# First stage of a four-stage decoder block kernel: a new order of a batch, and six of sixteen odd states summed by accumulating DMAs

## The reference, cut to what matters

```python
x = einsum('bld,ed->bel', hidden_states, in_proj_w)      # 512 channels
x = silu(causal_conv4(x) + conv_b)                       # u
dt_low, Bm, Cm = split(einsum('bdl,ed->bel', x, x_proj_w), [16, 32], axis=1)
dt = softplus(einsum('brl,dr->bdl', dt_low, dt_proj_w) + dt_proj_b)   # delta
def step(state, inp):                                    # 16 states a channel
    d, b, c, u = inp
    state = state * exp(d[..., None] * A) + (d * u)[..., None] * b[:, None, :]
    return state, einsum('bdn,bn->bd', state, c)
y = scan(step) + D[None, :, None] * x
y = y * silu(z)                                          # z is the layer-normalized input
```

## Time and profile before

| | |
|---|---|
| median of 3 runs | 3984.52 us (3982.64 to 3984.68) |
| the profiled execution's own time | 3983.86 us |
| its span | 3982.3 us |
| PE busy | 3702.0 us (93%) |
| DVE busy | 2985.4 us (75%) |
| ACT busy | 1753.5 us (44%) |
| POOL busy | 643.9 us (16%) |
| first scan of the first stage | starts at 62.8 us |
| DVE multiply L1763 that closes a batch | 256.95, ..., 646.40 and 804.93 us |

### The profile page before, as it was taken

How to read it: one execution, slowest core, us unless ns; L and a number is a source line. 1 busy time by engine, 2 the same in 40 slices (tenths; PEclk the granted TensorE clock), 3 DMA queues, 4 the chain that set the end, 5 groups by cost and what they waited for, 6 DMA issues and landing times.

```text
span 3982.3 us, 40913 instructions
## 1 busy us (share of the span) xinstructions
PE 3702.0 (93%) x12733; PEld 1922.2 (48%) x12786; DVE 2985.4 (75%) x4787; ACT 1753.5 (44%) x2732; POOL 643.9 (16%) x595
## 2 busy tenths in 40 slices
PE   7898898899999998899999999999999999999787
PEld 4555555544444444444446444455454455454343
DVE  5788888888979787888988655577377277377397
ACT  5767676742323323344342111155255255254276
POOL 2233232233434110244421000000000000000000
PEclk9999998999999999999999999999999999999898
DMA  4232222333242322434335000211011021021000
GB/s 139 76 108 78 102 96 82 139 139 137 82 160 100 119 79 91 162 143 161 126 109 227 22 22 21 88 65 66 29 65 57 29 74 52 32 71 70 0 11 32
DMA packets 91724, 344.89 MB, mean 87 GB/s; under 512 B 11776, under 2 KB 20096, under 8 KB 78112
## 3 DMA queue, kind: packets, MB, share of 16 engines
q1 hardware_dynamic: 63040, 230.05, 16.2%
q0 software_dynamic: 28512, 112.74, 8.4%
HBM read 280.36 MB, written 62.39 MB: 86 GB/s over the span
## 4 chain that ended last, share of the span: by engine, by line
PE 58%; DVE 22%; issue 11%; ACT 6%; DMA 2%; DVEq 0%; ACTq 0%; POOL 0%; SPq 0%; POOLq 0%
PE ps L1121 39%; PE ps L1499 5%; PE ps L1199 3%; PE ps L1330 3%; PE ps L1489 3%; PE ps L1382 3%; DVE room L1662 2%; DVE room L1666 2%; DVE room L1670 1%; ACT room L806 1%; DMA room<-bc_scratch 1%; PE ps L1189 1%; DVE stat L1626 1%; DVE room L1688 1%; DVE room L1675 1%
## 5 line engine op out<-in xcount | busy, mean ns | idle before, releaser
L1121 PE MATMUL ps<-room 128*128 128x512 bf16 (+2 forms) x3001 | 964.7, 478 | 54.7 <-DVE xres L2155 17.9
L1121 PE MATMUL ps<-lnT,room 128*128 128x512 f32 x2240 | 985.5, 595 | 23.5 <-DVE room L1871 15.1
L1121 PEld LDWEIGHTS ps<-lnT,room 128*128 128x128 f32 x2240 | 425.4, 191 | 567.7 <-issue 528.3
L1121 PEld LDWEIGHTS ps<-room 128*128 128x128 bf16 (+1 forms) x3040 | 422.1, 142 | 573.0 <-issue 318.5
L636 POOL TENSOR_TENSOR idle<-idle 128x1 f32<-128x1 f32 x268 | 468.2, 1747 | 1326.2 <-ACT room L816 508.6
L1330 PE MATMUL ps<-room 128*128 128x512 f32 x864 | 377.9, 595 | 7.3 <-DVE room L1822 7.3
L743 ACT ACTIVATE room<-room,small 128x511 f32<-128x511 f32 x256 | 163.6, 710 | 367.1 <-DVE room L1666 367.0
L1719 DVE TENSOR_TENSOR_SCAN room<-room 128x2048 f32<-128x2048 f32 x64 | 283.2, 4425 | 10.8 <-ACT room L806 4.7
L1666 DVE TENSOR_TENSOR_SCAN room<-room 128x2048 f32<-128x2048 f32 x64 | 283.4, 4428 | 5.4
L2115 DVE TENSOR_REDUCE stat<-ps 128x1 f32<-128x512 f32 x256 | 177.1, 692 | 132.1 <-PE ps L1121 132.1
L1330 PEld LDWEIGHTS ps<-room 128*128 128x128 f32 x864 | 164.2, 191 | 213.1 <-issue 207.3
(11 more groups left out here) (226 smaller groups left out, 4889.0 us busy)
## 6 DMA issues: line engine op xcount, KB each, us to landing
room<-in_ffn SPq DMA_DIRECT2D x16, 2048.0 KB, 10.6
room<-bc_scratch POOLq DMA_DIRECT2D x128, 256.0 KB, 3.6
room<-kv_stash SPq DMA_DIRECT2D x64, 512.0 KB, 3.4
kv_stash<-room POOLq DMA_DIRECT2D x96, 256.0 KB, 2.3
room<-stash POOLq DMA_DIRECT2D x24, 1024.0 KB, 5.6
room<-in_ffn SPq DMA_DIRECT2D x20, 1024.0 KB, 5.8
room<-in_ffn SPq DMA_DIRECT2D x12, 1536.0 KB, 7.5
room<-in_head SPq DMA_DIRECT2D x68, 256.0 KB, 3.7
```

What stands on the lines that cost most here:

```text
L1121: last = nc.tensor.matmul(out, lhsT, rhs, start=(i == 0), stop=(i == len(parts) - 1))
```

## The change

- **Order ahead of the loop.** SP loads the context and the first weight block before the small constants. Set 1's weights come after the key weights, and the delta weights have a semaphore of their own. x of the last batch is loaded only when the last batch begins. Columns of C are turned after delta is made. Only four units of keys and values are made ahead, one of them (2) before the first decay. Two one-column activations of Exp (`load_exp`) stand where the next real Exp is some work away.
- **Convolutions in pairs.** Two channel blocks go through all four taps, then the other two. `conv_done` and `u_ready` count to two each, silu and the 48-row projection follow by pairs.
- **Order in a batch.** On ACT the copies of state n come ahead of most side work of that n. Silu of set 1 and `take_xd` move to n = 2, the delta pieces and the Exp of set 1 one place earlier, silu of set 0 from n = 8 to 6, its Exp from 11 to 9, its Ln from 13 to 10, silu of z from 15 to 10. On DVE softplus of set 1 moves from 7 to 6, the convolution of set 0 from 5 to 6, the layer norm from 9 to 8, the delta*u pair from 10 to 9, softplus of set 0 from 12 to 10.
- **Keys and values.** Units sit at the states of `KV_ORDER`; two states (6 and 8) have two. Eight units use this batch's context from the loaded copy, four use the block loaded for the input projection. The last batch has eight units.
- **Single stores.** D*u is stored at n = 8, delta*u at 11, delta at 13, with a semaphore of its own for the first.
- **Accumulating DMAs.** States 1, 3, 5, 7, 9 and 11 are not summed on PE. Their turned copies go to one 1 MB buffer (`m_acc`: x's place for the last batch, or `m_nd` in the last batch), and POOL sends it to a DRAM tensor, the first as a plain store and the others with an addition. After state 12 POOL loads the sum back, and PE adds it with four matmuls at n = 14.

```diff
-KV_HEADS, KV_LEAD = 12, 6
+KV_HEADS, KV_LEAD = 12, 4
+ACC = (1, 3, 5, 7, 9, 11)
+ACC_LOAD, ACC_AT = 12, 14
+ACC_SUMMED = sum(n not in ACC for n in range(ACC_AT)) + 1
+SUMS = DS - len(ACC) + 1
+KV_OWN = KV_HEADS - KV_LEAD
+KV_ORDER = (4, 5, 6, 6, 7, 8, 8, 9, 10, 11, 12, 13)
...
+            sp.dma_start(ctx[:, :], ctx_d[0:P, :]).then_inc(ctx_loaded, 16)
+            sp.dma_start(mws[0][:, 0:MW], min_d[0:P, :]).then_inc(mw_loaded[0], 16)
             sp.dma_start(small[:, :], small_d).then_inc(small_loaded, 16)
...
+                    if last:
+                        sp.wait_ge(nsum_done, (B - 2) * SUMS + ACC_SUMMED)
+                        load_x(B - 1)
...
-                            sp.wait_ge(tile_filled, tile("kv", KV_HEADS - KV_LEAD - 1, 1)[0] + 1)
+                            sp.wait_ge(tile_filled, tile("kv", KV_OWN - 1, 1)[0] + 1)
                             sp.dma_start(m_kctx, ctx_d[bass.ds(b * P + P, P), :]).then_inc(kctx_loaded, 16)
...
+                        if n == 8:
+                            place = stashed(2, b)
+                            sp.wait_ge(Du_ready, b + 1)
+                            sp.dma_start(place, m_zT).then_inc(Du_stored, 16)
+                        if n in (11, 13):
+                            place = stashed((n == 11) * 1, b)
                             sp.wait_ge(stash_ready, b + 1)
+                            sp.dma_start(place, m_u2 if n == 11 else m_nd2).then_inc(stash_stored, 16)
...
-                sp.wait_ge(stash_stored, B * 48)
+                sp.wait_ge(stash_stored, B * 32)
+                sp.wait_ge(nsum_done, (B - 1) * SUMS + ACC_SUMMED)
+                sp.wait_ge(Du_stored, B * 16)
...
+                for n in range(DS):
+                    if n in ACC:
+                        if n > ACC[0]:
+                            pool.wait_ge(acc_added, b * (len(ACC) * 16) + ACC.index(n) * 16)
+                        wait(tile_taken, tile("h", n, NT - 1)[0] + 1, count)
+                        count += 1
+                        pool.dma_start(acc_stash, m_acc[last] if n % 2 else m_hT,
+                                       accum_op=ALU.add if n > ACC[0] else ALU.bypass).then_inc(acc_added, 16)
+                    for i in kv_slots(n, last):
+                        if i is not None:
+                            h = (KV_LEAD + i) % KV_HEADS
+                            place = kv_stashed(b + (1 if i >= KV_OWN else 0), h)
+                            store_unit(place, [tile("kv", i, half)[0] for half in range(2)], count,
+                                       None if last and i + 2 >= slots else (h + 2) % KV_HEADS, i)
+                            count += 2
+                    if n == ACC_LOAD:
+                        wait(acc_added, b * (len(ACC) * 16) + len(ACC) * 16, count)
+                        count += 1
+                        pool.dma_start(m_acc[last], acc_stash).then_inc(acc_loaded, 16)
...
+                    for pair in range(2):
+                        act.wait_ge(conv_done, 2 * f + (pair + 1))
+                        for e in (2 * pair, 2 * pair + 1):
+                            last_u = nc.scalar.activation(u3[:, e, :], u3[:, e, :], ACT.Silu, bias=cb[:, e:e + 1])
+                        last_u.then_inc(u_ready, 1)
...
+                        if n in (4, 5):
+                            take_dt(1, n - 4, tile)
+                        if n == 8 and not last:
+                            act.wait_ge(sp_corrected, front_b + 1)
+                        if n in (8, 9) and not last:
+                            take_dt(0, n - 8, tile)
+                        turned = t3(m_acc[last] if n in ACC and n % 2 else m_hT, NT)
+                        sent = sum(m in ACC for m in range(n - 1))
+                        if n - 2 in ACC and (n in ACC or n % 2 == 0):
+                            act.wait_ge(acc_added, b * (len(ACC) * 16) + sent * 16)
+                        for t in range(NT):
+                            i, bank = tile("h", n, t)
+                            act.wait_ge(tile_filled, i + 1)
+                            nc.scalar.activation(turned[:, t, :], ps[:, bank, :], ACT.Copy,
+                                                 scale=cT3[:, t, DR + DS + n:DR + DS + n + 1]).then_inc(tile_taken, 1)
+                        early, late = kv_slots(n, last)
+                        if early is not None:
+                            take_kv(early, b * (KV_HEADS * 16) + (KV_LEAD + early) * 16, tile)
+                        if n == 2:
                             silu_u(front_b, 1)
                             if not last:
                                 take_inproj(0, front_a, tile)
+                            take_xd(front_b, 1, b, tile)
                         if n == 5:
+                            exp_abs(1, tile)
+                        if n == 6 and not last:
+                            silu_u(front_a, 0)
+                        if late is not None:
+                            take_kv(late, b * (KV_HEADS * 16) + (KV_LEAD + late) * 16, tile)
                         if n == 6:
+                            ln_w(front_b)
+                            if not last:
+                                take_xd(front_a, 0, b + 1, tile)
...
+                        if n == 9 and not last:
+                            exp_abs(0, tile)
+                        if n == 10:
                             if not last:
+                                ln_w(front_a)
+                            act.wait_ge(Du_stored, b * 16 + 16)
                             for t in range(NT):
...
+                        if n == ACC_AT:
+                            pe.wait_ge(acc_loaded, b * 16 + 16)
+                            for t in range(NT):
+                                mm = nc.tensor.matmul(ps[:, t, :], ident[:, :], t3(m_acc[last], NT)[:, t, :], start=False, stop=False)
+                            mm.then_inc(nsum_done, 1)
+                        if n not in ACC:
+                            for t in range(NT):
+                                pe.wait_ge(tile_taken, tile("h", n, t)[0] + 1)
+                                mm = nc.tensor.matmul(ps[:, t, :], ident[:, :], hT3[:, t, :], start=(n == 0), stop=(n == DS - 1))
+                            mm.then_inc(nsum_done, 1)
...
-                    for j in range(DC - 1, -1, -1):
-                        for e in range(NE):
+                    for pair in range(2):
+                        for j in range(DC - 1, -1, -1):
+                            for e in (2 * pair, 2 * pair + 1):
...
                         if n == 2:
-                            dve.wait_ge(stash_stored, b * 48)
+                            dve.wait_ge(stash_stored, b * 32)
                             convolve(front_b, 1, tile)
-                        if n == 5 and not last:
-                            dve.wait_ge(Du_summed, b + 1)
-                            convolve(front_a, 0, tile)
-                        if n == 7:
+                        if n == 6:
                             softplus(front_b, 1)
+                            if not last:
+                                dve.wait_ge(Du_summed, b + 1)
+                                convolve(front_a, 0, tile)
```

More of the change, by code:

```diff
@@ L34, with kv_slots @@
 NBC = 2
[L37 to L44 removed]
+KV_HEADS, KV_LEAD = 12, 4
[5 more added lines that the diff above has]
+KV_ORDER = (4, 5, 6, 6, 7, 8, 8, 9, 10, 11, 12, 13)
+def kv_slots(n, last):
+    slots = [i for i, at in enumerate(KV_ORDER) if at == n and not (last and i >= KV_OWN)]
+    return (slots + [None, None])[:2]
 def mamba_tiles(last):
@@ L51, in mamba_tiles @@
     for n in range(DS):
+        early, late = kv_slots(n, last)
         names += [("h", n, t) for t in range(4)]
-        if kv_slot(n, last) is not None:
-            names += [("kv", kv_slot(n, last), half) for half in range(2)]
+        if early is not None:
+            names += [("kv", early, half) for half in range(2)]
         if n == 0:
@@ L652, in store_kv @@
                 tile = batch_tiles(b, last)
[L653 to L659 removed]
+                slots = KV_OWN if last else KV_HEADS
+                count = b * KV_WAITS + KV_FIRST
+                for n in range(DS):
[17 more added lines that the diff above has]
+                        pool.dma_start(m_acc[last], acc_stash).then_inc(acc_loaded, 16)
             def store_late(k):
@@ L1745, in body @@
                             v.tensor_tensor(m_u2, m_nd2, m_u2, ALU.mult).then_inc(stash_ready, 1)
-                        if n == 12 and not last:
+                        if n == 10 and not last:
                             softplus(front_a, 0)
```

192 lines of the change are left out of this document (83 added, 109 removed).

## The result

The changed kernel took **4008.56 us** (median of 4 runs, 4006.19 to 4014.7), the kernel before 3983.58 beside it: ratio **1.0068**, interval [1.0055, 1.008]. It is slower by 0.7% where 1.5% less was forecast; 4008.56 lies outside the range. The profiled execution took 4014.7 us, 0.15% above the median.

What follows compares the result with a forecast made beforehand. PE was taken as nearest to a bound, its lateness showing in DVE's waits. Gains of 14.7 ahead of the loop, 38.7 in three batches and 7 in the last sum to 60.4, giving 3923 us, range 3884 to 3974.

Steps and rivals of the forecast that it cites:

- The waits named above go: Loop batch: with sums taken off PE, four DVE waits totalling 25.4 us vanish, leaving 169.3 of 194.7 us at best.
- the closing 9.5: DVE's 9.5 us wait at L1763, closing a batch, for PE's last sums; claimed to go.
- the 4.8 for ACT's Ln of set 1: DVE's 4.8 us wait at L1743; claimed to go because that Ln moves three states ahead of its user.
- the 7.3 for row 11: DVE's 7.3 us wait for a row of B, read as PE's lateness through the context load; claimed to go.
- 181.8 - 6: Loop batch: forecast of 181.8 us, less the 6 us charged for the additions.
- +6.5, ACT late at the softplus of set 0: States 6 to 9: DVE waits 9.3 us for ACT's Exp, some 3 replacing an old wait, so 6.5 us a batch more.
- the new order does not do what it says: Rival, in the loop: batches stay near 194 us, only the stretch ahead and part of the last gained; 3964 us, chance 0.05.
- The additions, 9 us landing and 6 us a batch: POOL's queue: additions land in 9 us, key stores behind them delay ACT, costing 6 us a batch.
- The last batch, -7: Last batch: PE 11 us less, no ACT wait, 3 charged for the next stage's late weights; net gain 7 us.
- Ahead of the loop, 14.7 (9 to 18): Before the first scan: earlier weights, pairs, turned C after delta, Exp table and later keys together gain 14.7 us.
- the signs: Trace marks foretold: first scan at 48 us, L1763 some 182 apart, PE near 154, 88 sum records, row 11 unwaited.
- PE at its slower clock again the last releaser at L1763: Refuting sign at the batch's closing multiply; the others were additions beyond 14 us and ACT's copies waiting for acc_stash.

Runs made afterwards that it cites:

- e7: Changed kernel with the six odd states summed nowhere (missing from y) and no DMA for them; 3981.1 us, ratio 0.9989.
- e16: e9 with the sums of states 1, 3, 5, 7, 9 and 11 made nowhere, no DMA added; 3968.6 us, ratio 0.9962.
- e9: e3 with four leading units, late units reading the projection's context block, and the key context load at n = 14 instead of 10; 3960.8 us, ratio 0.9942.
- e1: Changed kernel with all sixteen states summed on PE and no accumulating DMAs; 3981.8 us, ratio 0.9998.
- e3: Kernel before with only the new stretch ahead of the loop and the pairs; old batch order, six leading units, no additions; 3964.5 us, ratio 0.9959.
- e5: Changed kernel with its additions turned into plain stores of the same size, so part of y is left out; 3992.9 us, ratio 1.0017.
- e8: Changed kernel with accumulating DMAs in the first three batches only, the last batch summing all states on PE; 3992.3 us, ratio 1.0016.
- e4: Changed kernel with the D*u store issued behind row 9 of B instead of ahead of it; 4006.0 us, ratio 1.0067.

## Why the prediction failed, step by step

- **The failed step is the first: "The waits named above go: 9.5 + 3.8 + 7.3 + 4.8 = 25.4, which leaves 194.7 - 25.4 = 169.3 us."** It took DVE's waits as things that PE's lateness causes one by one, and that leave when PE is 18.9 us lighter. e7 and e16 made PE that much lighter and more, with nothing added, and a batch stayed where it was (195.0 to 194.6, and 194.3 to 194.5). Term by term, in the order of before: the closing 9.5 is 9.03 us in e9 and 9.26 in e16, for PE makes the units and sums of states 14 and 15 there, none of which was taken off; the 4.8 for ACT's Ln of set 1 is 4.82 in e9 and 7.45 in e16; the 7.3 for row 11 went in e9 by the later context load and without any relief, and the batch kept its length. The waits' last releaser was PE, but what PE waited for was ACT (11.5 us before the key units in the trace of before, in the fence below; 10.1 and 12.7 before transposes and these units in e16), and ACT for PE (26.5 us for key units in the same batch of e16). The sums stand beside that ring: PE makes them while ACT takes what the ring handed it. The work on each engine says nothing of a cycle through both.

```profile
L1121 PE MATMUL ps<-down_rows,room 128*128 128x256 f32 x192 | 49.5, 416 | 11.5 <-ACT room L871 11.5
```

- **What the step weighs.** Without additions the forecast has 181.8 - 6 = 175.8 us a batch; e7, the new order with the relief and no DMA, has 200.8, 194.8 and 194.6. That is 63 us over three batches, of the 91 by which the profiled execution missed its forecast of 3923.5. Another 30 lie in the last batch (181.1 for 158.5 - 7).
- **"+6.5, ACT late at the softplus of set 0"**: the kind was right, the place and size were not. ACT is late at the softplus of set 1 already (10.22 us, at n = 6), then DVE waits at row 9 (6.69), whose load stands behind the D*u store, then 3.22 at the softplus of set 0. The forecast began its count at the end of scan 6 with ACT on time. The new order against the old one with the same stretch ahead of the loop costs 0.39%, 15.5 us in all (e1, e3). Against e9, which has four leading units too, half of the cost lies in the last batch (168.0 us for 157.2). The rival "the new order does not do what it says" described this and had a chance of 0.05. Even without additions its 3964 did not come (e1, 3981.8), because it counted on a gain in the last batch that turned into 9.5 us more than before.
- **The additions, 9 us landing and 6 us a batch.** The landing was well estimated (7.7, to 11.4), and so was the queue: the key store issued 0.7 us behind the addition at 716.41 landed after 7.5 us, with it, where it took 2.3 in the middle. The Trainium skill ("DMA: Bandwidth & Descriptors", Queues, rings and completion order) lets a later descriptor finish its write before an earlier one, but has the increment of the semaphore land only after every earlier write of that DMA engine; it says so of the queues of SP and ACT. The prediction used the first half alone. This store on POOL's queue agrees with the second: it did not pass the addition. ACT waited for key stores for 22.7 us in the four batches, 6.2 in e1; but e7, with no addition in the queue, has 20.5 and e5 3.8, so these waits do not measure what the additions cost. Stores, additions and read-backs together cost 0.79%, 31 us (changed kernel against e7), where 18 had been charged for three batches and nothing for the chain at the end of the last. In the traces the first three batches hold 13.4 us of it (603.6 for 590.2) and the last 11.3 (181.1 for 169.8).
- **The last batch, -7.** It became 22.5 us longer (158.5 to 181.1). The forecast priced PE's work and SP's weights (issued at 825.97 for 784.72, as foreseen after the sum at n = 14) and left out the one chain that has no other work beside it: the addition of state 11, the read-back, a late sum. DVE waits 12.61 us for it, and without it the batch takes 167.4 us (e8, 0.52% less in all). The rest was there without any DMA: 168.0 us in e1, with 9.90 us of waiting at the softplus of set 1 and 12.51 at row 9. That row is no simple price either: with the D*u store behind it (e4) the batch lost 3.4 us.
- **Ahead of the loop, 14.7 (9 to 18)**: 12.9, right. But in e3, with six units ahead of the loop, the first batch gave 13 of it back, and e9, with four leading units and the context load later, kept it (192.9 us); no run separates these two. The forecast charged and credited nothing for what the first batch inherits.
- Of the signs: sum records 88 as said; first scan 49.92 for 48; L1763 at 198 to 204 apart for 182; PE busy 165 for 154; row 11 waited for 2.95 instead of 7.3; ACT's copies never waited for `acc_stash`, and no addition landed beyond 14 us; "PE at its slower clock again the last releaser at L1763" came true (4.67, and 12.61 in the last batch), one of the three things that were to refute the sum.

What stays open: whether the ring of PSUM tiles is the bound, since no run loosened it; how much of the lost relief is the slower clock; and where in the loop the 11 us of the plain stores fall (the profiled execution of e7 was its slowest and differs from e5's by 1.2 us, the medians by 12). The rest of the kernel after this stage took 4 us longer in e9 than in e3, but in the 18 traces it runs from 3172 to 3186 us, so nothing follows from that.

## What to carry to other kernels

When the waits of one engine name a second as the last releaser, look at what the second waited for before counting its relief as a gain; two engines that hand a few buffers to and fro can bound the time with neither of them full, and leaving the work out of the computation for one run tells what its removal can give in that order. Where the longest wait is mended and the time stays, look for such a ring first, then mend the order. A transfer chained behind the last result (send, add, read back, use) has its whole latency on the path wherever no other work is left, so such a scheme should leave out the last round (e8: 0.52%).

## What the runs showed of the hardware that was not expected

- PE's relief turned partly into price: with six of sixteen sums left out the mean granted clock of the stretch fell from 0.95 to 0.89, and the same 256 transposes took 36.1 us for 33.8 and the same 128 matmuls of key units 37.9 for 33.0.
- An accumulating store of 1 MB to DRAM landed in 7.7 us in the middle (4.4 as a plain store), and a 256 KB store issued 0.7 us behind one on the same queue landed with it, in 7.5 for 2.3 us.
- The issue of an addition held POOL for 0.90 us, that of a plain store of the same bytes for 0.56.
